# Eight tiles of routing logits computed at attention's head, attention and dispatch in one block, transfers in another order, rows of x normed one pair later

## The chip, the cores and the metric

One NeuronCore of a Trainium2 chip runs the whole program. Its engines are TensorE (PE, with its weight loads shown as PEld), VectorE (DVE), ScalarE (ACT), GpSimd (POOL) and SyncE (SP, which here only issues DMAs). Each engine takes its own instructions strictly in order and waits on semaphores for the others. The metric is device time in microseconds, the median of several executions.

## The reference, cut to what matters

x is 4 x 2048 x 256 in float32. With xn = layernorm(x), the result is x + attention(xn) + soft_moe(xn).

```
# attention: 16 heads in 4 groups of keys and values, head size 16, causal
q, k, v = xn @ wq.T, xn @ wk.T, xn @ wv.T
att = softmax(mask(q . k / 4));  ctx = att . v;  out1 = ctx @ wo.T
# soft mixture of experts: 16 experts x 64 slots = 1024 slots
y        = layernorm(xn) * norm_g + norm_b
se       = (layernorm(slot_embeds) * slot_g + slot_b) * scale
logits   = y . se                            # per batch 2048 tokens x 1024 slots
dispatch = softmax(logits, over tokens);  combine = softmax(logits, over slots)
slots    = dispatch^T . y                    # 1024 x 256 per batch
eout     = (gelu(slots @ Wg + bg) * (slots @ Wu + bu)) @ Wd + bd
out2     = combine . eout
```

## The kernel before, in words

The program runs five stages: `project` (norms, q, k, v, and y transposed into `y_cols` in memory, with q, k, v and y_cols split into chunks of 512 tokens), `attend`, `dispatch`, `experts` and `combine`. Project, attend and dispatch each have a block of their own; at the end of a block all engines meet, and the next block begins with a jump on every engine (L152 after project, L698 after attend).

**Attend.** A group is one of 4 batches times one of 4 key and value groups, so there are 16. A group has 40 units (a chunk of 512 queries against 128 keys) and 160 maxes (matmuls of 128 queries x up to 512 keys, whose row maxima DVE reduces, L857 and L863; the exponents need them beforehand). A step is one unit of scores for 4 heads (L890), exponents on ACT (L809), the product with v two steps later (L932), and four maxes (L903) of the work 22 steps ahead (`LEAD`). The first 22 steps, -22 to -1, thus hold maxes alone: that is attention's head. Scores, maxes, the small transposes of the row maxima ("m", L909) and of the context ("c", L917) share a ring of seven PSUM banks, in order; PE may fill a bank once ACT or DVE has read what it held seven banks ago. At the head ACT fills unused rows of the queries and keys of groups 1 to 3 with zeros (L799, L801), and SP loads group 1 at step -6, group 2 at 6 and group 3 at 46.

**Dispatch.** The phases are L0, L1 (logits of batch 0 and 1), then for each batch the two halves of P (the sum over tokens), with L2 and L3 after P of batch 0 and 1. A tile of logits is 128 tokens x 1024 slots: 12 matmuls (L1246), because both operands are split into a high and a low part and three products are kept. ACT copies the tile out of PSUM (L1108), DVE takes its row maximum (L1166) and updates the column maximum (L1174), ACT makes the exponents over slots one tile later (L1081), and SP stores them to `slot_exps` (L1033). There are 16 tiles in a batch, 4 in a chunk of y_cols; three chunks fit (`RING`), SP loads the next one (L989), and POOL splits it into high and low (L1193, L1195). In the last six tiles of L1, L2 and L3, DVE also subtracts the column maximum from a half tile of the batch before (L1137), and ACT takes its exponent (L1061). ACT norms rows of x in pairs of tiles (L1071) for the P phases; four pairs fit.

The order is written out: `program(s)` gives the steps of attend and the lists in `dispatch` its phases. No scheduler reorders anything.

## Time and profile before

| | us |
|---|---|
| median of 3 runs | 2688.85 (2688.53 to 2691.77) |
| the profiled execution's own time | 2690.94 |
| its span, first to last instruction | 2689.2 |
| project | 0 to about 156 |
| attend | about 160.6 to 1758.5 |
| its head (maxes alone) | 160.6 to 203.9 |
| dispatch | 1761.0 to about 2206 |
| experts and combine | the rest |

The page gives PE as busy 96% of the span, DVE 76%, ACT 64%. Matmul ends are modelled, so PE at 9 or 10 tenths does not say that PE could do no more: a matmul's busy time includes its way through the array, and the start-to-start distance of matmuls is what tells their price. PEclk is the share of 2.4 GHz that was granted: 1.00 is 2.4 GHz, 0.50 is 1.2 GHz. A name in square brackets after an instruction is what it waited for.

### The profile page before, as it was taken

What the parts mean: (1) busy time and instruction counts of PE and PEld (TensorE: products, weight loads), DVE (VectorE), ACT (ScalarE), POOL (GpSimd) and SP (SyncE); (2) the same over time, 40 slices, a digit from 0 to 9 for tenths busy, and PEclk for the clock granted to TensorE, in tenths of its full rate; (3) what the DMA queues carried; (4) which work ended last, traced back from release to release, by engine and by line L of the source; (5) the groups of instructions that cost most, each with busy time, mean ns of one, the idle gap of its engine ahead of it and who ended that gap; (6) DMA issues with size and microseconds to landing.
All of it is one profiled execution on the core that took longest, in us unless ns stands there. A gap on an engine that the chain in (4) does not pass through costs nothing. (4 is left out here: it accounts for less than half of the span.)

```text
span 2689.2 us, 47797 instructions
## 1 busy us (share of the span) xinstructions
PE 2580.5 (96%) x16291; PEld 1541.4 (57%) x16291; DVE 2046.0 (76%) x4879; ACT 1728.3 (64%) x3510; POOL 429.8 (16%) x676
## 2 busy tenths in 40 slices
PE   7989999999999999999999999998989999999999
PEld 4444444444444444444444444367877888889999
DVE  8779989989999998998998898468475523356665
ACT  4577777778777777777777777867656651222221
POOL 6601111111111111111111111223130100100000
PEclk9968999999999999999999999999999999999999
DMA  7945423303312321330330000044333354545554
GB/s 255 309 116 64 54 34 45 45 11 42 45 21 30 45 33 17 45 45 6 45 45 6 8 8 29 9 174 173 125 130 145 102 187 141 172 155 194 194 192 150
DMA packets 175855, 245.10 MB, mean 91 GB/s; under 512 B 57205, under 2 KB 129017, under 8 KB 174105
## 3 DMA queue, kind: packets, MB, share of 16 engines
q1 hardware_dynamic: 160088, 227.73, 33.8%
q10 hardware_dynamic: 15552, 14.68, 1.8%
q8 instruction: 114, 1.87, 0.3%
q14 instruction: 101, 0.82, 0.1%
HBM read 156.21 MB, written 84.97 MB: 90 GB/s over the span
## 5 line engine op out<-in xcount | busy, mean ns | idle before, releaser
L809 ACT ACTIVATE att_pr<-att_ring 128x512 f32<-128x512 f32 (+3 forms) x2560 | 1174.3, 550 | 330.7 <-PE att_ring L890 323.8
L857 DVE TENSOR_REDUCE att_mx<-att_ring 128x1 f32<-128x512 f32 x1536 | 967.6, 680 | 75.5 <-PE att_ring L903 73.1
L903 PE MATMUL att_ring<-att_ks,att_qs 48*128 48x512 f32 (+3 forms) x1920 | 647.3, 422 | 16.3 <-ACT att_pr L809 6.8
L890 PE MATMUL att_ring<-att_qs,att_ks 64*128 64x512 f32 (+3 forms) x1920 | 576.3, 406 | 6.6 <-DVE att_mx L863 2.3
L890 PEld LDWEIGHTS att_ring<-att_qs,att_ks 64*128 64x128 f32 x1920 | 300.4, 186 | 401.8 <-DVE att_mx L857 145.2
L863 DVE CUSTOM_DVE_ANT_0 att_junk<-att_ring,w_causal 128x256 bf16<-128x256 f32 (+3 forms) x1024 | 466.1, 486 | 57.6 <-PE att_ring L903 31.2
L932 PE MATMUL att_acc<-att_pr,att_v 128*17 128x512 f32 (+3 forms) x3840 | 453.8, 544 | 2.7 <-ACT att_cT L820 1.5
L903 PEld LDWEIGHTS att_ring<-att_ks,att_qs 48*128 48x128 f32 x1920 | 307.1, 185 | 142.1 <-ACT att_pr L809 103.5
L760 POOL TENSOR_SCALAR_AFFINE_SELECT att_pr<-att_pr 128x512 f32<-128x512 f32 x256 | 162.5, 635 | 1031.4 <-ACT att_pr L809 1031.4
L903 PE MATMUL att_ring<-g_ks,g_qs 48*128 48x512 f32 (+3 forms) x640 | 227.7, 467 | 15.5 <-PEq L152 5.8
L1513 ACT CAST com_e1h<-com_tp 128x1024 fp32r<-128x1024 f32 x64 | 64.7, 1016 | 236.3 <-PE com_tp L1573 236.3
L890 PE MATMUL att_ring<-g_qs,g_ks 64*128 64x512 f32 (+3 forms) x640 | 199.5, 412 | 2.2 <-DVE att_mx L863 0.8
L1589 PE MATMUL com_mp<-pre_parts,com_e1h 128*128 x1024 | 186.4, 283 | 4.1 <-DVE com_e1l L1538 4.1
L890 PEld LDWEIGHTS att_ring<-g_qs,g_ks 64*128 64x128 f32 x640 | 104.3, 189 | 135.7 <-DVE att_mx L857 51.7
L1589 PEld LDWEIGHTS com_mp<-pre_parts,com_e1h 128*128 128x128 f32 x1024 | 158.5, 190 | 4.9 <-issue 4.9
L932 PE MATMUL att_acc<-att_pr,g_v 128*17 128x512 f32 (+3 forms) x1280 | 151.5, 545 | 0.0
L903 PEld LDWEIGHTS att_ring<-g_ks,g_qs 48*128 48x128 f32 x640 | 111.3, 203 | 67.6 <-ACT att_pr L809 28.2
L1589 PE MATMUL com_mp<-pre_parts,com_e1l 128*128 x512 | 144.7, 283 | 0.0
L932 PEld LDWEIGHTS att_acc<-att_pr,att_v 128*17 128x17 f32 x3840 | 78.2, 118 | 112.7 <-ACT att_pr L809 76.4
L1246 PE MATMUL dis_ps<-w_seTh,w_yTh 128*128 128x512 f32 x256 | 105.9, 414 | 20.1 <-ACT dis_lg L1108 9.1
L1263 PE MATMUL dis_ps<-dis_y,pre_parts 128*128 128x257 f32 x512 | 112.6, 381 | 4.4 <-ACT pre_parts L1061 4.4
L1263 PE MATMUL dis_ps<-dis_y,dis_lg 128*128 128x257 f32 x512 | 113.5, 384 | 3.0 <-ACT dis_lg L1061 3.0
(170 smaller groups left out, 3271.1 us busy)
## 6 DMA issues: line engine op xcount, KB each, us to landing
slot_exps<-dis_e SPq DMA_DIRECT2D x64, 512.0 KB, 2.7
com_e<-slot_exps SPq DMA_DIRECT2D x64, 512.0 KB, 3.5
att_qs<-q_parts SPq DMA_DIRECT2D x72, 256.0 KB, 12.0
q_parts<-proj_part SPq DMA_DIRECT2D x32, 512.0 KB, 5.0
dis_y<-in_L_attn_x_dram SPq DMA_DIRECT2D x64, 256.0 KB, 2.8
att_ks<-k_parts SPq DMA_DIRECT2D x72, 128.0 KB, 12.7
y_cols<-proj_yT SPq DMA_DIRECT2D x16, 512.0 KB, 5.3
context<-att_cn SPq DMA_DIRECT2D x64, 128.0 KB, 2.0
```

The lines of the kernel that those rows point to most:

```text
L760: nc.gpsimd.affine_select(out=blk, in_=blk, compare_op=ALU.is_ge, fill=0.0, base=0, pattern=[[0, GS], [1, P]], channel_multiplier=-1).then ...
L809: nc.scalar.activation(pr[:, s % NPR, h, off:CH], spot(("s", s, h)), ACT.Exp, scale=float(HD) ** -0.5).then_inc(exp_done, 1)
L857: nc.vector.tensor_reduce(dst, spot(e), AX.X, ALU.max).then_inc(mb_used, 1)
L863: nc.vector.tensor_tensor_reduce(junk[:, h % 2, 0:wd], spot(e), w["causal"][:, CH - wd:CH], 1.0, LOW, ALU.add, ALU.max, dst).then_inc(mb_u ...
L890: nc.tensor.matmul(spot(e), ks[g][r, kb * P:(kb + 1) * P], qs[g][r, c, hf * CH + off:(hf + 1) * CH], start=True, stop=True).then_inc(sT_re ...
L903: nc.tensor.matmul(spot(e), qs[g][r, c, q0:q0 + P], ks[g][r, j * CH:j * CH + wd], start=True, stop=True).then_inc(mb_ready, 1)
L932: last = nc.tensor.matmul(acc[VW * h:VW * h + HD + 1, off:CH], v[bg % NKV][:, kb // TPC, :, kb % TPC], pr[:, n % NPR, h, off:CH], start=(n ...
L1246: last = nc.tensor.matmul(ps[:, i % 2, 2 * (t % 2) + h, :], lhs[:, n % RING, k, (t % TPC) * P:(t % TPC + 1) * P], w[rhs][:, k, h * 512:(h ...
L1263: last = nc.tensor.matmul(ps[:, i % 2, q, 0:D + 1], lgs[b % 2][:, t, (hf * HB + q) * P:(hf * HB + q + 1) * P], y[:, m % NY, t % 2, 0:D + 1 ...
L1513: nc.scalar.copy(e1h[:, q].rearrange("p s n -> p (s n)"), tp[:, q, 0:2, :].rearrange("p a n -> p (a n)")).then_inc(e1h_kept, 1)
L1589: last = nc.tensor.matmul(mp[:, q, 0:D], lhs[:, q, s, :], rhs[:, b, s, :], start=(s == 0 and rhs is eoh and lhs is e1h), stop=(s == SB - 1 ...
```

## The change

Six things change together.

1. **Eight tiles at the head.** The first 8 tiles of L0 (`NE`), in 16 halves of 128 x 512, are computed in steps -17 to -2 of attend, one half at the end of each step: six matmuls into one bank of the ring. ACT copies the half into a slot of `pr` and issues its store to a new array `first_logits`. Before that, SP loads two chunks of y_cols and POOL splits them. ACT's zeros are cut into pieces of 2048: six before the steps, twelve more one behind each of the halves 0 to 11. ACT waits for the first 12 stores at step 0 and for the last 4 at step 3.
2. **Their maxima.** In the last group SP loads the eight tiles back, to where dispatch wants them; DVE does their row and column maxima in attend's last 28 steps, where no maxes are left. L0 of dispatch then has tiles 8 to 15 only.
3. **One block.** Attend and dispatch share a block. In place of the meeting of all engines PE waits for each bank's last reader, and ACT waits before its third exponent tile until the contexts are stored.
4. **Exponents.** The 32 exponent tiles of L0 and L1 are spread over the 24 tiles of logits that are left, with four buffers in place of two.
5. **Transfers.** The loads of groups 1 and 2 move from steps -6 and 6 to -2 and 10, and the first waits until the first 12 halves are stored. In dispatch the chunk of y_cols is loaded after the exponents of a chunk's fourth tile are stored, no longer before those of its third.
6. **Rows of x** are normed one pair later in the P phases. The queries of all groups lie in one tensor, which project's `part` now shares.

```diff
+NE = 8
-    FIRST_LOADS = {-6: 1, 6: 2, 46: 3}
+    FIRST_LOADS = {-2: 1, 10: 2, 46: 3}
+    NL = 2 * NE
+    L_FROM = -LEAD + 5
+    L_LATE = NL - GS
...
+        early = [("l", s - L_FROM)] if 0 <= s - L_FROM < NL else []
-        out = [st[0], xs[0], st[1], xs[1]] + ev + [xs[2], st[2], st[3], xs[3]] + av
+        out = [st[0], xs[0], st[1], xs[1]] + ev + [xs[2], st[2], st[3], xs[3]] + early + av
...
 # SP
+            for n in range(NEC):
+                sp.dma_start(cols["low"][:, n].bitcast(F32), scr["yT_in"][0, n]).then_inc(cols["in"][n], 16)
                 for s in ALL_STEPS:
                     if s in FIRST_LOADS:
+                    sp.wait_ge(l_out, 16 * L_LATE)
                         load_first(FIRST_LOADS[s])
...
+                if s == STEPS - NU + AV_LAG:
+                    sp.wait_ge(pv_done, (NBG - 4 + -(-NE // 4)) * NU)
+                    for t in range(NE):
+                        sp.dma_start(lg[:, t, :], scr["first_logits"][t]).then_inc(l_in, 16)
...
 # ACT
+            for k in range(NRG * ZP):
+                zero_rows(k)
                 for s in ALL_STEPS:
+                for e in program(s):
+                    if e[0] == "l":
+                        act.wait_ge(mb_ready, turn[e] + 1)
+                        nc.scalar.copy(half_tile(e[1]), spot(e)).then_inc(l_kept, 1)
+                        if e[1] < (NKV - 2) * NRG * ZP:
+                            zero_rows(NRG * ZP + e[1])
+                        act.dma_start(scr["first_logits"][t, :, h * 512:(h + 1) * 512],
+                                      half_tile(e[1])).then_inc(l_out if e[1] < L_LATE else l_late, 16)
+                if s == 0:
+                    act.wait_ge(l_out, 16 * L_LATE)
+                if s == NPR - 1:
+                    act.wait_ge(l_late, 16 * (NL - L_LATE))
...
 # PE
+                    elif e[0] == "l":
+                        wait_bank(pe, e)
+                        pe.wait_ge(l_split, 2 * (t // TPC) + 2)
+                        for k in range(DK):
+                            nc.tensor.matmul(spot(e), hi, seTh[:, k, to], start=(k == 0), stop=False)
+                            nc.tensor.matmul(spot(e), hi, seTl[:, k, to], start=False, stop=False)
+                            last = nc.tensor.matmul(spot(e), lo, seTh[:, k, to], start=False, stop=(k == DK - 1))
...
 # dispatch
+        first_tile = lambda b: 0 if b else NE
+        SLOTS = 2 * TPB - NE
+        exps_by = lambda b, t: min(-(-2 * TPB * (b * TPB + t + 1 - NE) // SLOTS), b * TPB + t)
...
-                            norm_rows(half_of(ph) * PAIRS + (t + 1) // 2 + 2)
+                            norm_rows(half_of(ph) * PAIRS + (t + 1) // 2 + 1)
```

On PE at the head, steps -19 to -14, where `att_ring` is a bank of the ring: before,

```order
L903 MATMUL att_ring<-g_ks,g_qs 128x512 x2
L903 MATMUL att_ring<-g_ks,g_qs 128x256 x2
L903 MATMUL att_ring<-g_ks,g_qs 128x512 x6
L909 MATMUL att_ring<-w_ident,att_nml 32x128
L903 MATMUL att_ring<-g_ks,g_qs 128x384 x2
```

and now, the maxes being L977, the first transpose of row maxima L994 and a half tile of logits the six matmuls L986 to L988:

```order
L977 MATMUL att_ring<-g_ks,w_queries 128x512 x4
L986 MATMUL att_ring<-w_seTh,w_yTh 128x512
L987 MATMUL att_ring<-w_seTl,w_yTh 128x512
L988 MATMUL att_ring<-w_seTh,w_yTl 128x512
L986 MATMUL att_ring<-w_seTh,w_yTh 128x512
L987 MATMUL att_ring<-w_seTl,w_yTh 128x512
L988 MATMUL att_ring<-w_seTh,w_yTl 128x512
L977 MATMUL att_ring<-g_ks,w_queries 128x512 x2
L994 MATMUL att_ring<-w_ident,att_nml 32x128
L977 MATMUL att_ring<-g_ks,w_queries 128x384 x2
```

Six matmuls stand behind the four maxes of each step from -17 on, and the transpose stands behind the first half tile.

On ACT, from attend's first instruction: before, all zeros and then the first exponents,

```order
L799 CAST att_qs<-w_causal 32x4096
L801 CAST att_ks<-w_causal 32x2048
L799 CAST att_qs<-w_causal 32x4096
L801 CAST att_ks<-w_causal 32x2048
L799 CAST att_qs<-w_causal 32x4096
```

and now, where L840 are the zeros, L848 the copy of a half tile and L853 its store:

```order
L840 CAST w_queries<-w_causal 32x2048 x2
L840 CAST att_ks<-w_causal 32x2048
L840 CAST w_queries<-w_causal 32x2048 x2
L840 CAST att_ks<-w_causal 32x2048
L848 COPY att_pr<-att_ring 128x512
L840 CAST w_queries<-w_causal 32x2048
L853 DMA first_logits<-att_pr 128x512
L848 COPY att_pr<-att_ring 128x512
L840 CAST w_queries<-w_causal 32x2048
L853 DMA first_logits<-att_pr 128x512
```

A copy that frees a bank of the ring stands behind a piece of zeros twelve times.

On PE where attend ends and dispatch begins, before:

```order
L932 MATMUL att_acc<-att_pr,att_v 17x512 x4
L917 MATMUL att_ring<-w_ident,att_cT 128x128 x4
L698 UNCONDITIONAL_BRANCH
L1211 UNCONDITIONAL_BRANCH
L1246 MATMUL dis_ps<-w_seTh,w_yTh 128x512
```

and now:

```order
L1017 MATMUL att_acc<-att_pr,att_v 17x512 x4
L1002 MATMUL att_ring<-w_ident,att_cT 128x128 x4
L1348 UNCONDITIONAL_BRANCH
L1385 MATMUL dis_ps<-w_seTh,w_yTh 128x512
```

The end of the block has gone; a jump within the block is left. The first matmul of dispatch is now that of tile 8.

## Rows read from the trace of the kernel before

**Rows 1.** The page's busy times by engine.

```profile
PE 2580.5 (96%) x16291; PEld 1541.4 (57%) x16291; DVE 2046.0 (76%) x4879; ACT 1728.3 (64%) x3510; POOL 429.8 (16%) x676
```

**Rows 2.** Busy time of each engine by stretch, around attention's head.

```profile
core 0: us, PE busy (x) PEld busy (x) DVE busy (x) ACT busy (x) POOL busy (x), PEclk, DMA share, GB/s
...
200.00:205.00 5.00, 4.99 (x11) 2.41 (x10) 5.00 (x13) 0.31 (x1) 0.00 (x0) 0.50 1.11 126
...
215.00:220.00 5.00, 5.00 (x36) 2.30 (x33) 5.00 (x14) 3.97 (x9) 0.63 (x1) 0.90 0.02 5
```

**Rows 3.** Timeline of the head's first part: start, duration, instruction, wait.

```profile
160.59 3.60 ACT L799 CAST att_qs<-w_causal 32x4096 fp32r<-32x4096 f32 x1 [4.99 <-PEq L152]
...
164.10 1.89 ACT L801 CAST att_ks<-w_causal 32x2048 fp32r<-32x2048 f32 x1
...
169.04 0.20 POOL L778 CAST att_nml<-att_nm 128x16 fp32r<-128x16 f32 x1 [8.21 <-DVE att_nm L831]
```

**Rows 4.** Timeline of the head's second part and of step 0.

```profile
170.68 0.39 PE L909 MATMUL att_ring<-w_ident,att_nml 128*32 128x128 f32 x1
...
190.72 2.46 DVE L857 TENSOR_REDUCE att_mx<-att_ring 128x1 f32<-128x512 f32 x4
...
192.14 0.40 SPq L528 DMA_DIRECT2D att_qs<-q_parts  x1
...
203.89 0.76 PE L890 MATMUL att_ring<-g_qs,g_ks 64*128 64x512 f32 x1
```

**Rows 5.** Timeline where attend ends and dispatch begins.

```profile
1755.71 0.58 ACT L820 COPY att_cT<-att_acc 128x512 f32<-128x512 f32 x1 [1.19 <-PE att_acc L932]
1756.44 0.63 PE L917 MATMUL att_ring<-w_ident,att_cT 128*128 128x128 f32 x4 [0.80 <-ACT att_cT L820]
...
1761.02 0.77 PE L1246 MATMUL dis_ps<-w_seTh,w_yTh 128*128 128x512 f32 x1 [3.95 <-PEq L698]
...
1761.58 0.63 PE L1246 MATMUL dis_ps<-w_seTl,w_yTh 128*128 128x512 f32 x1
...
1762.01 0.63 PE L1246 MATMUL dis_ps<-w_seTh,w_yTl 128*128 128x512 f32 x1
...
1766.01 0.40 PE L1246 MATMUL dis_ps<-w_seTh,w_yTh 128*128 128x512 f32 x1
...
1766.71 0.40 PE L1246 MATMUL dis_ps<-w_seTh,w_yTh 128*128 128x512 f32 x1
```

**Rows 6.** Timeline of L0: one tile's period on ACT and DVE.

```profile
1777.41 1.01 ACT L1108 COPY pre_parts<-dis_ps 128x1024 f32<-128x1024 f32 x1 [0.65 <-PE dis_ps L1246]
...
1778.32 1.15 ACT L1081 ACTIVATE dis_e<-pre_parts,dis_nr 128x1024 f32<-128x1024 f32 x1
...
1779.37 0.19 ACT L1081 ACTIVATION_READ_ACCUMULATOR dis_e<-pre_parts,dis_nr 128x1 f32 x1
...
1780.21 1.02 ACT L1108 COPY pre_parts<-dis_ps 128x1024 f32<-128x1024 f32 x1 [0.65 <-PE dis_ps L1246]
...
1790.80 3.37 DVE L1174 TENSOR_TENSOR dis_cm<-dis_cm,pre_parts 128x1024 f32<-128x1024 f32 x1
```

**Rows 7.** Busy times by stretch: attend's end, and L0.

```profile
1720.00:1730.00 10.00, 8.46 (x72) 2.89 (x68) 0.00 (x0) 10.00 (x25) 3.51 (x4) 1.00 0.00 1
...
1780.00:1790.00 10.00, 10.00 (x44) 8.05 (x43) 8.66 (x8) 7.84 (x11) 3.50 (x2) 1.00 0.66 259
```

**Rows 8.** DMA issues, whole run: queue, count, KB, median us to landing.

```profile
slot_exps<-dis_e SPq DMA_DIRECT2D x64, 512.0 KB, 2.7
...
w_yTl<-y_cols SPq DMA_DIRECT2D x16, 512.0 KB, 4.2
...
proj_x<-in_L_attn_x_dram ACTq DMA_DIRECT2D x12, 512.0 KB, 5.3
```

**Rows 9.** DMA issues between 160 and 230.

```profile
context<-att_cn SPq DMA_DIRECT2D x1, 128.0 KB, 15.0
```

**Rows 10.** Waits between 1862 and 1980: us in total, times, longest.

```profile
ACT dis_y L1071 <- DMA dis_y<-in_L_attn_x_dram: 13.6, 10, 2.0
```

More of the change, by code:

```diff
@@ L99, in project @@
         x = a.sb("x", [P, NX, TPC, D])
+        room = queries[:, QW:]
+        part = room[:, 0:12 * CH].rearrange("p (q s h n) -> p q s h n", q=2, s=3, h=2)
         xn = a.sb("xn", [P, 2, TPC, D])
@@ L537, in load_ones, with attend @@
             yield sp.dma_start(ks[row:row + 1, :].bitcast(F32), w["ones"][0:S // 64, :].bitcast(F32)).then_inc(ones_set, 16)
-def attend(nc, w, scr, g0, cols):
+def attend(nc, block, w, scr, g0, cols, queries, first_logits):
     def chunk_units(c):
@@ L642, in place @@
             spot[1] += need
-        return where, before, {e: m[-1] for e, m in mates.items()}
+        return where, before, {e: m[-1] for e, m in mates.items()}, held
     NEAR = 4
     fills = [e for s in ALL_STEPS for e in program(s) if e[0] != "a"]
-    where, before, last_mate = place(fills)
+    where, before, last_mate, held_last = place(fills)
     turn = {e: n for n, e in enumerate(e for e in fills if e[0] != "s")}
@@ L653, in attend @@
         passed = a.sem("passed")
-        qs = [g0["qs"]] + [a.sb(f"qs{g}", [P, CPB, HL * CH], F32R) for g in range(1, NKV)]
+        qs = [queries[:, g * QW:(g + 1) * QW].rearrange("p (c n) -> p c n", c=CPB) for g in range(NKV)]
         ks = [g0["ks"]] + [a.sb(f"ks{g}", [P, S], F32R) for g in range(1, NKV)]
@@ L942, in dispatch, with bank_free, stored @@
+        def bank_free(pe, bank):
+            if bank < NBANK:
+                wait_read(pe, held_last[bank])
+            else:
+                pe.wait_ge(cT_ready, NBG * CPB)
+        def stored(eng):
+            for c in range(CPB):
+                eng.wait_ge(c_out[c], 16 * NBG)
+        return bank_free, stored
+def dispatch(nc, block, w, io, scr, pre, cols, first_logits, before):
     HB = SB // 2
@@ L976, in dispatch @@
         NYP = B * 2 * PAIRS
+        first_tile = lambda b: 0 if b else NE
+        SLOTS = 2 * TPB - NE
+        exps_by = lambda b, t: min(-(-2 * TPB * (b * TPB + t + 1 - NE) // SLOTS), b * TPB + t)
+        WIDE = 2 * TPB
+        place = lambda n: n % 4 if n < WIDE else n % 2
+        stores_before = lambda n: n // 4 if n < WIDE else (WIDE // 4) + (n - WIDE) // 2
         def tiles_of(m):
@@ new lines, in _, with split, column_maxes @@
+        @block.gpsimd
+        def _(pool):
+            def split(n):
+                if n < B * CPB:
+                    q = n % RING
+                    wait_apart(pool, yT_in[q], 16 * ((n - NEC) // RING), passed)
+                    nc.gpsimd.tensor_copy(yTh[:, q], yTl[:, q].bitcast(F32)).then_inc(yT_high, 1)
+                    pool.wait_ge(yT_high, n - RING - NEC + 1)
+                    nc.gpsimd.tensor_tensor(yTl[:, q], yTl[:, q].bitcast(F32), yTh[:, q].bitcast(F32),
+                                            ALU.subtract).then_inc(yT_split, 1)
+            def column_maxes(b):
+                wait_apart(pool, cm_done, TPB * (b + 1), passed)
+                for hf in range(2):
+                    h = slice(hf * 512, (hf + 1) * 512)
+                    nc.gpsimd.partition_all_reduce(cm[:, b % 2, h], cm[:, b % 2, h], P, RMAX).then_inc(ca_ready, 1)
+            for b in range(B):
+                if b:
+                    column_maxes(b - 1)
+                for n in range(b * CPB if b else NEC, b * CPB + CPB):
+                    split(n + RING)
+            column_maxes(B - 1)
@@ L1640, in block_kernel @@
                 "in": [a.sem(f"yT_in{n}") for n in range(RING)]}
+        first_logits = {"nr": a.sb("nr", [P, 2, TPB]), "cm": a.sb("cm", [P, 2, NS]),
+                        "nr_ready": a.sem("nr_ready"), "cm_done": a.sem("cm_done")}
+        with ExitStack() as place:
+            parts = Alloc(nc, place, "pre").sb("parts", [P, 2, B, SB, D], F32R)
+        lg = parts[:].bitcast(F32).rearrange("p a b s d -> p (a b s d)").rearrange("p (t n) -> p t n", n=NS)
+        first_logits["lg"] = lg
+        both = ExitStack()
         with ExitStack() as early:
             b = Alloc(nc, early, "w")
+            queries = b.sb("queries", [P, NKV * QW], F32R)[:]
             w["causal"] = b.sb("causal", [P, CH])
@@ L1650, in block_kernel @@
                 load_ones(sp, w, g0["ks"], g0["ones_set"]))
-            project(nc, w, io, scr, g0)
-            attend(nc, w, scr, g0, cols)
+            project(nc, w, io, scr, g0, queries)
+            block = both.enter_context(nc.Block())
+            before = attend(nc, block, w, scr, g0, cols, queries, first_logits)
         with ExitStack() as late:
             b = Alloc(nc, late, "pre")
-            parts = b.sb("parts", [P, 2, B, SB, D], F32R)
+            b.sb("place", [P, 2 * B * SB * D])
             high, low = parts[:, 0].bitcast(F32), parts[:, 1].bitcast(F32)
@@ L1670, in block_kernel @@
                    "parts": parts}
-            dispatch(nc, w, io, scr, pre, cols)
+            with both:
+                dispatch(nc, block, w, io, scr, pre, cols, first_logits, before)
             com = combine_inputs(late, nc, io, scr)
```

1055 lines of the change are left out of this document (552 added, 503 removed).

## The prediction

> **What bounds the kernel now.** I read the page's busy times first [rows 1]: PE is busy 96% of the span. That is an average; what eight tiles are worth where they stand now, and what they cost where they go, has to be read at those two places.
>
> The first is L0. In the timeline [rows 6] ACT's copies of two tiles in a row start at 1777.41 and 1780.21, and each ends a wait on PE of 0.65. So a tile takes 2.80 us and PE sets it: 12 matmuls, one each 0.233 (the 13th and the 16th matmul of dispatch start at 1766.01 and 1766.71, 0.70 for three) [rows 5]. ACT's part of a tile is a copy of 0.91 (1777.41 to 1778.32) and exponents of 1.24 (1778.32 to 1779.56), together 2.15. DVE is busy 8.66 of 10 us there [rows 7].
>
> The second is attention's head. In the stretches [rows 2] DVE is busy 5.00 of 5 us between 200 and 205 while the granted clock is 0.50, the 1.2 GHz level; PE reads 4.99, but with only 11 matmuls in 5 us, each waiting for DVE to read a bank. DVE needs 2.46 for four full maxes [rows 4]. So at the head DVE sets the time and PE, at half clock, has room. Between 215 and 220 the clock comes back (0.90) once scores, maxes and products stand close together. The third place is the border of attend and dispatch [rows 5]: the last transposes end at 1757.07, and dispatch's first matmul starts at 1761.02 after 3.95 us in which PE's sequencer waited at the block's end. From there the clock is at half again: matmuls two and three start 0.43 apart (1761.58, 1762.01).
>
> **The change part by part.**
>
> *Taken out of L0.* Eight tiles by 2.80 = 22.4 us, all on the path, since PE sets L0.
>
> *The border.* Without the meeting PE goes on at 1757.07 when it has had its transposes; the banks it fills first were read by exponents that are over by then. 1761.02 - 1757.07 = 3.9 us. At least a jump remains, so between 0 (the engines' sequencers need the time anyway) and 3.9; I take 3.9, as nothing else is shown in the gap. The first tile's 12 matmuls took 4.99 (1761.02 to 1766.01) in place of 2.80; with no gap in PE's work the clock should stay: 2.2 us more, or 0 if the short waits at attend's end bring it down all the same. So dispatch gives back 22.4 + 3.9 + 2.2 = 28.5.
>
> *The exponents of L0 and L1.* 32 tiles over 24 is 4/3 a tile: ACT 0.91 + 4/3 x 1.24 = 2.56 a tile, still under 2.80. A tile with two exponents takes 3.39 on ACT, its neighbours 2.15, and PE has two tiles of PSUM to run ahead in. Cost 0, but the cover has shrunk from 0.65 to 0.24 us a tile. The stores grow to 512 KB every 2.1 us while the DMA engines are 0.66 busy [rows 7], about 0.85; with four buffers and 2.7 us to landing [rows 8] that holds. Bounds: 0 to 0.5 a tile over 16 tiles, 8 us.
>
> *Maxima of the eight tiles.* 16 operations on DVE of the kind that took 3.37 beside POOL [rows 6] and about a third of it alone, some 20 to 30 us with POOL beside a few of them, in a stretch where DVE is busy 0.00 of 10 and ACT 10.00 [rows 7]. Hidden. Behind them on DVE stands one copy of row maxima, for a chunk of scores four steps later. The load back, 4 MB, is issued in the last group's first steps, some 16 steps before DVE's maxes run out. 0, at most 2.
>
> *The head, the term that costs.* Before, the m transpose, behind 26 maxes, starts at 170.68 and step 0, behind 88, at 203.89 [rows 4]: 62 maxes in 33.2 us, 2.14 a step of four. Now:
> - Half tile 0 comes before that transpose, at half clock: 6 x 0.43 = 2.6 us.
> - The next step is ten matmuls at half clock, 4.3, so 2.2 more than 2.14. By then PE has worked without a gap for about as long as in dispatch's first tile, where the clock was back after 5 us [rows 5], and I take full clock from there.
> - 14 more steps. PE at full clock needs 10 x 0.233 = 2.33 at most. ACT, in ten of the 14, has a copy of 0.58 (the same shape) [rows 5] and a piece of zeros of 1.76 to 1.89 (3.51 from 160.59 to 164.10 for 4096 columns; 1.89 for 2048) [rows 3], together 2.4. DVE's share stays 2.14. So 2.4 against 2.14: 14 x 0.26 = 3.6.
> - POOL's two splits (a cast and a subtraction each) stand before its part in the m transpose, which it did at 169.04 [rows 3]. They begin when the chunk is there, about 4.2 us after 160.6 [rows 8]. PE needs the first split at about 169.5, where half tile 0 stands. 0 to 3 us; I take 0, since PE at half clock is late there anyway.
> Sum 2.6 + 2.2 + 3.6 = 8.4. Below, it can't be under 14 x (2.33 - 2.14) = 2.7; above, see the first rival. In return steps 0 to 5 run at full clock. They lie before 216 with DVE nearly always busy [rows 2]: 0 to 2.5 us back, I take 1.5.
>
> *Other moves.* Group 1's load was issued at 192.14 [rows 4], is now issued about 15 us later, and is needed at step 18, so 18 steps of 2.14 or more after step 0: hidden. The later norming takes ACT's waits for rows of x away (13.6 us in ten waits) [rows 10], in phases where PE was busy throughout; against that, three pairs in place of two are normed in the middle of L2 and L3. 0, between -2 and 2. The chunk of y_cols loaded one tile later still has two chunks' time: 0.
>
> Sum: -28.5 + 8.4 - 1.5 = -21.6. From the profiled execution, 2690.94 (span 2689.2), that is 2669.3; it was 2.1 above the median 2688.85, so 2667.
>
> The Trainium skill speaks against the head term: TensorE: Matmul & The Clock Gate, in "A second HAM failure mode: psum-queue depth-cycling", says that a PE which idles briefly between groups of matmuls as it goes round PSUM banks can have its clock swing between the two levels. The trace agrees for the head as it was (0.50 with 4.99 of 5 us busy) and not for attend as a whole, where the same ring runs at 1.00 in the stretches shown of its end [rows 7]. By that rule the head would be the first rival.
>
> **The rivals.**
> - *The clock stays at half through the head; slower.* For it: at the head it was 0.50 though PE read busy for 4.99 of 5 us, and PE still waits for ACT and DVE once a step [rows 2]. Against: at half clock ten matmuls need 4.3 us and nothing else needs more, so PE would have no gap, and without gaps it came back within 5 us at 1761 [rows 5]. Price: 16 steps of 4.3 in place of 2.14 is 34.6, and nothing back in steps 0 to 5: -28.5 + 34.6 = +6, 2695. It decides from about 14 of the 16 steps at half clock.
> - *ACT holds up the head's end.* The last four halves are stored while group 1's load runs; a context store of 128 KB took 15.0 us to land in such a stretch [rows 9], and ACT waits for these four at step 3. With 15 to 20 us to landing step 3 waits some 10: 2677. For: these rows. Against: that store stood in SP's own queue, and on ACT's queue 512 KB landed in 5.3 [rows 8]. The Trainium skill, DMA: Bandwidth & Descriptors, "Queues, rings and completion order", says that a DMA engine takes turns between queues packet by packet; by that the wait is 0, and no row here shows both at once for these shapes.
> - *ACT or the stores become the bound of L0 and L1.* 3.3 a tile in place of 2.8 over 16 tiles: +8, 2675. For: cover of 0.24 us only, DVE 87% busy. Against: four buffers.
> - *The border stays.* A jump and fetching of instructions cost the 3.9, and the clock falls as before, 2.2: 2673.
> - *The head hides nearly all.* 2.7 in place of 8.4: 2661.
>
> **How the numbers follow.** Forecast 0.50 at 2667, its own range 2662 to 2673. Half clock at the head 0.07; late stores 0.09; L0 and L1 bound elsewhere 0.12; the border 0.09; the head hidden 0.13. The range of 2656 to 2680 takes in the last three and most of the stores, and leaves the first out. A measurement of this kernel tells 0.2% (5.4 us) from no change: under 2683.5 is faster. All but the first rival lie below it; for several of them at once I move some chance: faster 0.87, within 0.2% 0.05, slower 0.08.
>
> **What would show it.** In the profile after: the granted clock in 5 us stretches from 169 on, 0.50 until about 175 and then near 1.00; the first score matmul at 211 to 213 (before 203.89); ACT's copies of half tiles 2.4 apart; no wait of ACT at step 3. Dispatch's first matmul within 0.5 us of attend's last transposes, at full clock, about 7 us later on the clock of the span than 1757; tiles of L0 2.80 apart; the first matmul of P some 22 us earlier than before. The prediction is wrong if the head's end lies past 220, or if the tiles of L0 are more than 3 us apart.

## The result, and the profile after

The changed kernel takes 2676.5 us (median of 7 runs, 2669.35 to 2685.1); the kernel before, run beside it, 2688.85 (7 runs, 2686.45 to 2691.77). The ratio is 0.9954, with a 95% interval of 0.9939 to 0.9968: faster by 0.46%, about 12 us. The forecast was 2667; 2676.5 lies inside the range of 2656 to 2680, but 9.5 us above the likeliest case. The profiled execution has a span of 2677.9 against 2689.2, 11.3 less, and all readings below are of these two. The page's busy times, against [rows 1]:

```profile
span 2677.9 us, 47844 instructions
PE 2569.2 (96%) x16291; PEld 1530.4 (57%) x16291; DVE 2037.7 (76%) x4879; ACT 1729.7 (65%) x3524; POOL 428.3 (16%) x676
```

As before they name no culprit. The span has to be cut at events that both kernels have: ACT's first piece of zeros, step 0's first score, attend's last transposes, dispatch's first matmul, the first and the last product.

| stretch | before | after | difference | forecast |
|---|---|---|---|---|
| to the first zeros | 160.6 | 161.0 | +0.4 | 0 |
| head: to step 0's first score | 43.3 | 48.5 | +5.2 | +8.4 |
| steps of attend, to the end of the last transposes | 1553.2 | 1565.3 | +12.1 | -1.5 |
| border, to dispatch's first matmul | 3.95 | 0.48 | -3.5 | -3.9 |
| L0 and L1, to the first product | 99.5 | 78.9 | -20.6 | -24.6 |
| first to last product (both P of 0 to 3, L2, L3) | 343.3 | 337.4 | -5.9 | 0 |
| the rest | 485.3 | 486.3 | +1.0 | 0 |

One row is off by 13.6 us, and against it all others together are 3.3 us better than forecast: the head and the products gave more (3.2 and 5.9), L0 and L1 4.0 less. The timeline of that stretch (start, duration, engine, line, and in brackets the idle time before it and what ended it) answers to [rows 4]:

```profile
209.46 0.43 PE L964 MATMUL att_ring<-w_queries,g_ks 64*128 64x512 f32 x1
...
226.44 0.94 ACT L865 ACTIVATE att_pr<-att_ring 128x256 f32<-128x256 f32 x3 [9.04 <-DMA first_logits<-att_pr]
...
226.97 0.76 PE L964 MATMUL att_ring<-w_queries,g_ks 64*128 64x512 f32 x1 [6.21 <-ACT att_pr L865]
```

Step 0 starts at 209.46, 5.6 later than before. Then ACT waits 9.04 us for stores of half tiles, and PE waits for ACT. The stretches around it answer to [rows 2] (busy time, instructions, granted clock, DMA share, GB/s):

```profile
core 0: us, PE busy (x) PEld busy (x) DVE busy (x) ACT busy (x) POOL busy (x), PEclk, DMA share, GB/s
210.00:215.00 5.00, 4.22 (x17) 2.11 (x17) 4.99 (x15) 2.95 (x8) 0.64 (x1) 0.96 1.01 160
215.00:220.00 5.00, 5.00 (x25) 1.95 (x22) 4.08 (x10) 1.92 (x5) 1.69 (x4) 0.50 1.04 184
220.00:225.00 5.00, 0.75 (x10) 0.16 (x8) 1.53 (x4) 0.00 (x0) 0.00 (x0) 0.50 1.06 157
225.00:230.00 5.00, 3.03 (x13) 1.30 (x17) 1.98 (x4) 2.79 (x7) 0.63 (x1) 0.50 0.39 28
```

Between 220 and 225 every compute engine stands still or nearly so; only the DMA engines work. The clock was at half before that, from 215, where PE had 25 matmuls in 5 us and mostly waited for DVE's maxes. The last four stores of half tiles (ACT's queue, from 204.4 to 209.7), as the trace has them:

```profile
L853 ACTq DMA_DIRECT2D first_logits<-att_pr x4: 326/334/346, 204.4 to 209.7; - x4
  ACT att_pr L865: 9.0, 1
DMA to landing us min/median/max: 6.6/13.5/16.7
```

The border answers to [rows 5]:

```profile
1774.17 0.63 PE L1002 MATMUL att_ring<-w_ident,att_cT 128*128 128x128 f32 x4 [0.80 <-ACT att_cT L876]
1774.84 0.39 ACT L832 COPY att_cc<-att_ring 128x272 f32<-128x272 f32 x1 [0.81 <-PE att_ring L1002]
1775.28 0.50 PE L1385 MATMUL dis_ps<-w_seTh,w_yTh 128*128 128x512 f32 x1 [0.48 <-ACT att_cc L832]
1775.62 0.40 PE L1385 MATMUL dis_ps<-w_seTl,w_yTh 128*128 128x512 f32 x1
1775.85 0.39 PE L1385 MATMUL dis_ps<-w_seTh,w_yTl 128*128 128x512 f32 x1
```

The meeting is gone and the matmuls are 0.23 apart from the second on. What is left, 0.48, is a wait that the prediction did not name: the first matmul needs the bank that ACT's copy reads (the prediction had the first banks free by then). In L1, at 1820 to 1829:

```profile
1820.38 1.02 ACT L1243 COPY dis_lg<-dis_ps 128x1024 f32<-128x1024 f32 x1 [0.65 <-PE dis_ps L1385]
...
1823.57 4.04 ACT L1193 ACTIVATE dis_y<-dis_y,w_yb,w_ys 128x256 f32<-128x256 f32 x8
1827.51 0.99 ACT L1243 COPY dis_lg<-dis_ps 128x1024 f32<-128x1024 f32 x1
...
1828.56 0.50 PE L1385 MATMUL dis_ps<-w_seTh,w_yTh 128*128 128x512 f32 x1 [2.61 <-ACT dis_lg L1243]
```

The tiles ahead of it are on average as in [rows 6], 2.80 apart (copies at 1809.18 and 1811.98); a tile with two exponents takes 3.19 and the one behind it 2.41. These two copies are 7.13 us apart: between them two exponents and the four pairs of rows of x in one piece, and PE waits 2.61 for it.

### The profile page after: what moved, and what is told of

Its sections match the earlier page's. It is cut to its first block and busy times, and to the rows that moved or that the text cites. A ratio compares the mean times of both kernels' runs of the same rounds, so it can differ in the third digit from the quotient of the medians.

```text
span 2677.9 us, 47844 instructions
## 1 busy us (share of the span) xinstructions
PE 2569.2 (96%) x16291; PEld 1530.4 (57%) x16291; DVE 2037.7 (76%) x4879; ACT 1729.7 (65%) x3524; POOL 428.3 (16%) x676
## 5 line engine op out<-in xcount | busy, mean ns | idle before, releaser
L977 PE MATMUL att_ring<-att_ks,w_queries 48*128 48x512 f32 (+3 forms) x1920 | 647.4, 422 | 16.9 <-ACT att_pr L865 8.1
L964 PE MATMUL att_ring<-w_queries,att_ks 64*128 64x512 f32 (+3 forms) x1920 | 576.5, 407 | 7.4 <-DVE att_mx L937 2.3
L964 PEld LDWEIGHTS att_ring<-w_queries,att_ks 64*128 64x128 f32 x1920 | 300.8, 186 | 403.5 <-DVE att_mx L931 144.6
L977 PEld LDWEIGHTS att_ring<-att_ks,w_queries 48*128 48x128 f32 x1920 | 307.2, 185 | 142.5 <-ACT att_pr L865 103.8
L977 PE MATMUL att_ring<-g_ks,w_queries 48*128 48x512 f32 (+3 forms) x640 | 212.7, 440 | 11.5 <-PEq L156 5.8
L964 PE MATMUL att_ring<-w_queries,g_ks 64*128 64x512 f32 (+3 forms) x640 | 200.2, 413 | 9.0 <-ACT att_pr L865 6.2
L964 PEld LDWEIGHTS att_ring<-w_queries,g_ks 64*128 64x128 f32 x640 | 104.4, 189 | 144.0 <-DVE att_mx L931 54.0
L977 PEld LDWEIGHTS att_ring<-g_ks,w_queries 48*128 48x128 f32 x640 | 101.3, 193 | 58.6 <-ACT att_pr L865 28.2
L1385 PE MATMUL dis_ps<-w_seTh,w_yTh 128*128 128x512 f32 x224 | 92.9, 415 | 19.9 <-ACT dis_lg L1243 13.0
## 6 DMA issues: line engine op xcount, KB each, us to landing
w_queries<-q_parts SPq DMA_DIRECT2D x96, 256.0 KB, 12.1
```

What stands on the lines that cost most here:

```text
L964: nc.tensor.matmul(spot(e), ks[g][r, kb * P:(kb + 1) * P], qs[g][r, c, hf * CH + off:(hf + 1) * CH], start=True, stop=True).then_inc(sT_re ...
L977: nc.tensor.matmul(spot(e), qs[g][r, c, q0:q0 + P], ks[g][r, j * CH:j * CH + wd], start=True, stop=True).then_inc(mb_ready, 1)
L1385: last = nc.tensor.matmul(ps[:, i % 2, 2 * (t % 2) + h, :], lhs[:, n % RING, k, (t % TPC) * P:(t % TPC + 1) * P], w[rhs][:, k, h * 512:(h ...
```

## The experiments

There are twelve kernels. "Early load" in the later ones is the edit of the second. Behind "Measured" stand the median, the lowest and highest run, and the ratio to the kernel before with its 95% interval; the kernel before had 2689.1, 2689.5 and 2690.2 in the three sets. Theory A, for the row that is off by 13.6: the last four stores stand behind group 1's load on the DMA engines, ACT waits, and PE's clock is back late.

A stretch is read from one execution of each kernel, and kernels with the same code in a stretch show how far that can be trusted. The steps of attend, by what each kernel does there:

| attend | step 0's first score to step 20's | all steps |
|---|---|---|
| as before (before, e4_before_norm1) | 51.0, 51.0 | 1553.2, 1558.6 |
| with ACT's wait at step 3 (changed, e3_norm2, e5_two_blocks, e8_yT_order) | 60.7, 57.9, 58.0, 59.1 | 1565.3, 1560.0, 1563.5, 1563.2 |
| without it (the other eight) | 50.3 to 54.2 | 1550.6 to 1558.9 |

All steps differ by 5 us within one row; the first twenty tell the three rows apart. So the wait and the half clock behind it cost the changed kernel 9.7 of its 12.1, and 7 to 8 in the other three, where ACT waited 8.1, 8.2 and 6.6. The other 2.4 lies behind step 20, where short pieces of half clock fall differently in each execution (13.6 us at 0.50 against 10.3 before).

**e1_hold.** The load held back until the stores have landed.

```
                 if s in FIRST_LOADS:
                     sp.wait_ge(l_out, 16 * L_LATE)
+                    sp.wait_ge(l_late, 16 * (NL - L_LATE))
                     load_first(FIRST_LOADS[s])
```


> The changed kernel, but SP also waits for the last four stores of halves before it issues group 1's load (the load starts some 8 us later). Theory A (the stores queue behind that load): the last four stores land in 2 to 5 us, ACT's wait of 9.04 us before step 3 goes, step 3 no longer stands still at 222 to 226, attend's end comes 9 to 12 us earlier, about 2667. Rival B (stores of 256 KB from ACT's queue take about 15 us whatever runs beside them): the wait stays at 8 to 10 us, 2676. Rival C (the wait goes, but the clock is at half through steps 0 to 10 in any case, since DVE bounds them): the wait goes and only 5 to 7 us come back, 2670.

Measured: 2671.75 (2664.16 to 2677.98), ratio 0.9932 (0.9906 to 0.9957). The last four stores, and the stretches after step 0:

```profile
L854 ACTq DMA_DIRECT2D first_logits<-att_pr x4: 326/326/327, 202.9 to 208.2; - x4
DMA to landing us min/median/max: 2.0/2.1/2.5
```
```profile
215.00:220.00 5.00, 5.00 (x30) 1.80 (x30) 4.08 (x11) 2.27 (x7) 1.19 (x4) 0.50 1.11 121
220.00:225.00 5.00, 4.96 (x25) 1.67 (x23) 3.76 (x9) 3.21 (x7) 0.51 (x1) 0.67 0.95 104
225.00:230.00 5.00, 5.00 (x37) 2.32 (x36) 4.85 (x11) 4.46 (x11) 0.64 (x1) 1.00 1.13 125
```

The same 256 KB from the same queue land in 2.1 us in place of 13.5: rival B (15 us whatever runs beside) falls. The wait is gone, and attend's steps take 1552.7 in place of 1565.3. The first twenty steps give back 8.7 of that (52.0 against 60.7); the other 3.9 lies behind them, where the code is the same, in short pieces of half clock. The clock falls to 0.50 at 215 here too, as rival C has it, and is back at 1.00 after 225, where with the wait it was still 0.50. The median moved by 4.8, to 2671.75: theory A had the cause right and its 9 to 12 us were too much, and rival C, with 5 to 7 us and 2670, came nearest to the time. Single runs of one kernel are 14 us apart.

**e2_early_load.** The load ahead of the late stores.

```
-    FIRST_LOADS = {-2: 1, 10: 2, 46: 3}
+    FIRST_LOADS = {-14: 1, 10: 2, 46: 3}
                 if s in FIRST_LOADS:
-                    sp.wait_ge(l_out, 16 * L_LATE)
                     load_first(FIRST_LOADS[s])
```


> The changed kernel, but group 1's load is issued at step -14 instead of -2 and does not wait for the stores, so it runs beside stores 2 to 11 and the last four stores have the DMA engines to themselves. Theory A: those early stores land late (10 to 17 us) but nobody waits for them before step 0; the wait before step 3 goes, 9 to 12 us earlier, about 2667. Rival B (stores always take 15 us): 2676. Rival D: the wait only moves, to step 0, where ACT waits for twelve stores: 2 to 6 us there, 2671.

Measured: 2671.69 (2665.4 to 2676.69), ratio 0.9931 (0.9909 to 0.9952). No wait at step 3, none at step 0 (rival D falls); the stores around step 0 land in 2.0 at the median and 4.9 at most; all steps take 1555.5, the first twenty 50.6. Two different edits that part stores and load do the same.

**e11_in_turn.** Stores and load at the same time, but a short backlog.

```
+                for i, _ in enumerate(itertools.chain(load_group(...), load_ones(...))):
+                    if g == 1 and i % 3 == 2:
+                        sp.wait_ge(loaded[g], 16 * (i + 1))
```


> The changed kernel, but SP has at most three transfers of group 1's load under way: it waits for each three to land before it issues the next. Theory A1 (a store waits for all that is queued on the DMA engines ahead of it, whichever queue it came from): with a short backlog the late stores land in 2 to 7 us although the load still runs beside them, ACT's wait before step 3 goes, 2667 to 2671. Theory A2 (the engines share packet by packet between the two queues for as long as both have work): the load runs beside them as before, the stores take 10 us or more, the wait stays at 5 to 10 us.

Measured: 2671.3 (2664.67 to 2674.51), ratio 0.9924 (0.9909 to 0.9939). Landing of the last four stores, and the stretches in which load and stores are both under way:

```profile
L855 ACTq DMA_DIRECT2D first_logits<-att_pr x4: 326/326/326, 205.0 to 210.3; - x4
DMA to landing us min/median/max: 2.1/3.7/6.8
```
```profile
210.00:215.00 5.00, 4.21 (x18) 2.08 (x15) 5.00 (x12) 2.70 (x6) 0.64 (x1) 0.94 0.82 159
215.00:220.00 5.00, 5.00 (x26) 2.05 (x23) 4.23 (x12) 2.44 (x7) 1.70 (x4) 0.50 0.69 105
220.00:225.00 5.00, 4.93 (x38) 2.31 (x36) 4.80 (x12) 3.90 (x9) 0.64 (x1) 0.88 0.64 92
```

Two of these four stores were issued before the load began and landed in 2.3 and 2.1; the two beside it, with three transfers under way, landed in 6.8 and 5.2, in place of 12.5 to 16.7. ACT does not wait, step 3 goes on, and the first twenty steps take 52.2. So what made the stores late was how much SP had issued, 17 transfers in ten us, though it stood in another queue.

A1's 2 to 7 us came and A2's 10 or more did not. But that does not settle how the engines divide their time between the queues, since beside a short load a shared engine is soon free too, and the packets speak for each theory in turn. In the changed kernel, between 215 and 222, the load's queue (q1) and that of the stores (q10) moved the same number of packets (packets, MB, share of 16 engines' time):

```profile
q1 hardware_dynamic: 235, 0.81, 68.9%
q10 hardware_dynamic: 239, 0.45, 34.4%
```

That is A2, packet by packet: the load's packets are the larger ones and take most of the time, and the stores move 0.45 MB in 7 us, where in e11_in_turn they moved 0.48 MB in the 2 us before the load (206 to 208). But in e11_in_turn, between 208 and 212, the store issued at 208.0 hardly moves while the three transfers issued ahead of it do, which is A1:

```profile
q1 hardware_dynamic: 160, 0.59, 103.0%
q10 hardware_dynamic: 4, 0.01, 1.0%
```

So a store can wait for what was issued ahead of it, and it can share the engines with the load. What decides between the two stays open.

**e5_two_blocks.** The border alone undone.

```
-            with both:
+            both.close()
+            with nc.Block() as block:
                 dispatch(nc, block, ...)
```


> The changed kernel with attend and dispatch in two blocks again, as before; all else as changed. If the border term was sized right: 3.5 to 4 us between attend's last transposes and the first matmul of logits in place of 0.5, and 2.2 us more in the first tile at half clock, so 5 to 6 us slower than the changed kernel, about 2682. Rival: a jump costs the same in one block and the gain came from the eight tiles alone: within 1 us in the stretch from the last transposes to the third tile.

Measured: 2681.17 (2675.3 to 2692.78, 12 runs), ratio 0.9972 (0.9958 to 0.9987), 4.7 above the changed kernel.

```profile
1771.71 0.63 PE L1002 MATMUL att_ring<-w_ident,att_cT 128*128 128x128 f32 x4 [0.80 <-ACT att_cT L876]
...
1774.59 0.77 PE L1385 MATMUL dis_ps<-w_seTh,w_yTh 128*128 128x512 f32 x1 [2.26 <-PEq L1821]
1775.15 0.63 PE L1385 MATMUL dis_ps<-w_seTl,w_yTh 128*128 128x512 f32 x1
1775.58 0.63 PE L1385 MATMUL dis_ps<-w_seTh,w_yTl 128*128 128x512 f32 x1
```

The meeting costs 2.26 here (less the 0.48 of the joined block 1.8 net), less than the 3.95 before: the block's end no longer waits for the context's last store, since SP's wait for it now stands in dispatch. Before, that store was issued at 1758.50 and landed at 1760.47, and PE went on 0.55 later; here it was issued at 1773.77 and PE went on at 1774.59, before it landed at 1775.64. And the matmuls are 0.43 apart, the clock at half: the first twelve take 5.26 against 2.91, 2.4 more. 1.8 + 2.4 = 4.2, and the medians say 4.7. (L0 and L1 as a whole take 81.6 against 78.9, but seven kernels with the same code there lie between 76.9 and 81.7, so that stretch does not show it.) The border is real, and its price in the kernel before had three parts, of which one was the wait for a store. The joined block does not always keep the clock: in e10_all, e11_in_turn and e12_early_norm2 it was at half there as well, without a meeting, and the first twelve matmuls took 3.8 to 3.9.

**e8_yT_order.** The chunks of y_cols loaded where they were.

```
+                        if t % TPC == TPC - 2:
+                            load_yT(b * CPB + t // TPC + RING)
                         store_exps(exps_by(b, t) if b < 2 else b * TPB + t + 1)
-                        if t % TPC == TPC - 1:
-                            load_yT(b * CPB + t // TPC + RING)
```


> The changed kernel with the chunks of y_cols loaded where they were before, one tile earlier and ahead of the exponents' stores. The prediction priced this move at 0 with two chunks of time in hand. If so: within 1.5 us of the changed kernel in the stretch of L0 and L1 and in L2 and L3. If SP now waits for a chunk's last tile with finished exponents behind it: ACT waits for free buffers in L0 and L1, 2 to 6 us slower.

Measured: 2677.03 (2672.15 to 2678.37), ratio 0.995 (0.9931 to 0.9968); L0 and L1 78.6 (78.9), first to last product 337.5 (337.4). No effect, as forecast.

**e3_norm2, e12_early_norm2, e4_before_norm1.** The later norming: undone in the changed kernel, undone with the early load, and done alone in the kernel before.

```
-                            norm_rows(half_of(ph) * PAIRS + (t + 1) // 2 + 1)
+                            norm_rows(half_of(ph) * PAIRS + (t + 1) // 2 + 2)
```


> The changed kernel with the rows of x normed two pairs ahead again, as before. The phases from the first product to the last logits took 5.9 us less after the change than before. If the later norming is worth that (ACT no longer waits for rows of x in front of exponents that PE needs): 3 to 6 us slower than the changed kernel. If it comes from another part (which cores of the block's queue, clock): within 1.5 us of it.

> The kernel with group 1's load issued early, and the rows of x normed two pairs ahead as before the change. The profile of the changed kernel with that (343.4 us from the first to the last product, against 337.4) said 6 us, its median 2678 against 2676.5 said 2. If the later norming is worth 5 to 6: that stretch takes 340 or more against 334.4, and the median is 2675 to 2678. If it is worth 2 or less: the stretch is under 338 and the median 2671 to 2674.

> The kernel before with only the norming of rows of x one pair later. If the later norming is worth 3 to 6 us by itself: 2683 to 2686. If not: 2687 to 2690. If it only helps together with the new order of transfers, this run is at 2689 while the run without it is slower than the changed kernel.

| kernel | pairs ahead | median | first to last product |
|---|---|---|---|
| changed | 1 | 2676.5 | 337.4 |
| e3_norm2 | 2 | 2678.28 | 343.4 |
| e2_early_load | 1 | 2671.69 | 334.4 |
| e12_early_norm2 | 2 | 2672.21 | 339.2 |
| before | 2 | 2689.09 | 343.3 |
| e4_before_norm1 | 1 | 2689.47 | 342.2 |

With two pairs ahead the stretch is longer in each pair of rows, by 6.0, 4.8 and 1.1; the medians differ by 1.8, 0.5 and -0.4, and the interval of the last (0.9977 to 1.0007) holds no change. Part of the difference between the profiles is where short pieces of half clock fell in that one execution: in e1_hold, with the same code there, the stretch is 338.3. One part of it is free of that: the P phases of batches 2 and 3, at full clock in every run, take 115.6 or 115.7 in the three kernels with two pairs ahead and 114.7 in all nine with one (e9_skew and e10_all, which change more, left out), e4_before_norm1 too. So 1.0 us is shown. What the later norming is worth in the other phases, up to 6 us in all, these runs don't settle. ACT's waits for rows of x over that stretch (us in total, times, longest; the first part of it before stands in [rows 10], the whole had 56.9 in 43 waits) do shrink, but most of what went was not on the path:

```profile
ACT dis_y L1193 <- DMA dis_y<-in_L_attn_x_dram: 38.0, 30, 2.1
```

**e7_zeros_pool.** ACT's part of the head moved.

```
-                        if e[1] < (NKV - 2) * NRG * ZP:
-                            zero_rows(NRG * ZP + e[1])
+                    if m < 2:            # GpSimd, behind its parts of the first two m
+                        for k in range(NRG * ZP * (m + 1), NRG * ZP * (m + 2)):
+                            ...
+                            nc.gpsimd.tensor_copy(rows, w["causal"][r, 0:1].to_broadcast([32, S])).then_inc(zeroed[g], 1)
```


> The kernel with group 1's load issued early, and the twelve pieces of zeros that stand behind half tiles 0 to 11 on ACT moved to GpSimd. If ACT (copy and zeros) sets the head's steps at 2.53 us: steps become 2.33 (ten matmuls at full clock), and step 0's first score comes about 2.4 us earlier. If matmuls with their waits set them: the spacing of the half tiles stays at 2.5. If GpSimd beside DVE makes DVE's maxes slower: 2.6 or more.

Measured: 2668.17 (2660.64 to 2670.28), ratio 0.9911 (0.9889 to 0.9933). From the second half tile's copy to the last one: changed kernel 175.9 to 209.1, 33.2, with eleven spacings of 2.53; here 177.1 to 208.8, 31.7. The 2.53 was ACT's (copy, zeros and the issue of a store), but when the zeros end PE is up to 1.5 us ahead in its banks, and the next copies follow 1.0 and 2.0 apart: only 1.5 us were on the path. The head as a whole was not shorter (48.7 from first zeros to first score against 48.5), since in this execution the clock stayed at half through 175 (0.50 in 170:175, 0.65 in 175:180; changed kernel 0.63 and 1.00). The early load, with the same late clock, had 50.1.

**e6_spread_norms.** The 4.04 us in one piece divided.

```
-                        if b >= 1 and t == 7:
-                            norm_rows(2 * (b - 1) * PAIRS + NY)
+                        if b >= 1 and t < 8 and t % 2:
+                            norm_rows(2 * (b - 1) * PAIRS + (t + 1) * NY // 8)
```


> The kernel with group 1's load issued early, and in L1 the four pairs of rows of x normed one at a time behind tiles 1, 3, 5 and 7 in place of all four behind tile 7. If those 4.04 us in one piece, on an ACT that is 96% busy there, are what lost 4 us in L0 and L1: the stretch from the first matmul of logits to the first product takes 76 to 77 us in place of 80 to 81, and the run is some 4 us under the one with the early load alone, 2668. If ACT's work as a whole is the bound there (exponents of 32 tiles behind 24 tiles): the stretch stays within 1 us of 80.

Measured: 2669.29 (2666.29 to 2672.17), ratio 0.9925 (0.9906 to 0.9943). L0 and L1 take 77.7 against 80.3 with the early load alone. That is inside the spread of kernels with the same code there (76.9 to 81.7), but the place shows it: from the tenth copy behind dispatch's first matmul to the eighteenth it is 23.7 in place of 26.0. So 2.3 of the 4 us that were missing, and the medians say 2.4.

The last six tiles of L1 remained, 4.5 us apart in every kernel, and before the change as well. One period in the changed kernel:

```profile
1838.91 0.99 ACT L1243 COPY dis_lg<-dis_ps 128x1024 f32<-128x1024 f32 x1
...
1839.94 1.22 DVE L1303 TENSOR_REDUCE w_nr<-dis_lg 128x1 f32<-128x1024 f32 x1 [1.60 <-ACT dis_lg L1243]
1841.08 1.21 DVE L1311 TENSOR_TENSOR w_cm<-w_cm,dis_lg 128x1024 f32<-128x1024 f32 x1
1842.21 0.69 DVE L1272 TENSOR_TENSOR pre_parts<-pre_parts,w_cm 128x512 f32<-128x512 f32 x1
1842.93 0.63 ACT L1183 ACTIVATE pre_parts<-pre_parts 128x512 f32<-128x512 f32 x1 [1.88 <-DVE pre_parts L1272]
1843.46 0.99 ACT L1243 COPY dis_lg<-dis_ps 128x1024 f32<-128x1024 f32 x1
```

Neither engine is full: DVE idles 1.60 for ACT and ACT 1.88 for DVE, in turn. The exponents of the slots (L1183) need this tile's subtraction on DVE, and stand on ACT ahead of the next tile's copy.

**e9_skew.** Those exponents one tile later.

```
-                        if b >= 1 and t >= TPB - AHEAD:
-                            exp_tile(b - 1, t - (TPB - AHEAD))
+                        if b >= 1 and t > TPB - AHEAD:
+                            exp_tile(b - 1, t - (TPB - AHEAD) - 1)
...
                         token_exps(b * TPB + TPB)
+                        exp_tile(b - 1, AHEAD - 1)
```


> The kernel with group 1's load issued early, and in the last six tiles of L1, L2 and L3 the exponents of the slots on ACT stand one tile later, behind the next tile's copy. In L1 these tiles stand 4.5 to 4.6 us apart, while ACT has some 3.4 and DVE 3.4 a tile: copy, then DVE's two maxima and its subtraction, then exponents, then the next copy, one behind the other. If that loop sets them: 3.4 to 3.6 apart, 5 to 6 us less in each of L1, L2 and L3, and the run at 2654 to 2658. If the clock (0.66 in the stretches 1827:1832 and 1837:1842 of such a kernel) sets them: still 4.5 apart, 2671.

Measured: 2648.98 (2647.2 to 2651.77), ratio 0.9847 (0.9833 to 0.9862), 22.7 under the early load alone.

```profile
1829.75 1.00 ACT L1242 COPY dis_lg<-dis_ps 128x1024 f32<-128x1024 f32 x1
...
1831.36 0.68 DVE L1272 TENSOR_TENSOR pre_parts<-pre_parts,w_cm 128x512 f32<-128x512 f32 x1
...
1832.08 0.63 ACT L1182 ACTIVATE pre_parts<-pre_parts 128x512 f32<-128x512 f32 x1 [0.19 <-DVE pre_parts L1272]
1832.61 1.00 ACT L1242 COPY dis_lg<-dis_ps 128x1024 f32<-128x1024 f32 x1
```

The copies are 2.86 apart in place of 4.55. L0 and L1 take 70.2 (80.3), first to last product 323.2 (334.4): 21.3 together, more than the 15 to 18 expected. In L2 and L3 both kernels are at full clock, so that the loop alone gave the 3.6 (49.4 against 53.0) and 4.2 (47.9 against 52.1) there; in L1 it gave 10.1, with 6.8 us at half clock gone as well. The rival named the clock as the cause; it came back with the loop's end. From 1829.2 to 1843.2 it is 1.00, where the changed kernel has 0.88.

**e10_all.** Early load, zeros on GpSimd, divided norms, later exponents.

> Group 1's load early, the twelve pieces of zeros on GpSimd, the four pairs in L1 normed one at a time, and the exponents of the slots one tile later. If the parts add: 1.5 (zeros), 2 (pairs) and 15 (exponents) under the 2671.7 of the early load alone, about 2653. If the pairs' gain is the same slack of ACT that the later exponents free: 2655 to 2657.

Measured: 2643.92 (2640.11 to 2645.87), ratio 0.9828 (0.9814 to 0.9842): the best version, 1.7% under the kernel before and 32.6 us under the changed one. L0 and L1 take 70.0, as with the later exponents alone, so the divided norms add nothing to them. It is 5 us under e9_skew, whose values, 2647.2 to 2651.77, don't meet these. The profiled executions are 8.9 apart, and that lies in attend: the head takes 46.1 in place of 48.8, and the steps 1550.6 in place of 1557.0. In the steps e10_all was at half clock for 11.2 us and e9_skew for 27.3. In e2_early_load and e12_early_norm2, with the same attention code as e9_skew, 20.5 and 28.1 us at half clock go with 1555.5 and 1558.9, which is 0.4 to 0.5 us for each; at that price the clock is the whole difference of the steps. The early load's two kernels agree: 13.7 us at half clock and 1551.8 with the zeros on GpSimd, 20.5 and 1555.5 with them on ACT. Whether the zeros on GpSimd keep the clock or chance did stays open.

## Why the prediction was right, and where it was wrong

- **Direction and range** were right, on the terms of L0 and the border. The likeliest case was not what happened: it was the second rival. That its 2677 met 2676.5 is in part luck: the row of attend's steps came out 3.6 above that rival's sum and L0 and L1 4.0 above it, and the head and the products made up for it by 3.2 and 5.9.
- **The step that failed** is the late stores, "on ACT's queue 512 KB landed in 5.3": the prediction made of it a wait of 0. The choice between that row and the 15.0 of a store in such a stretch [rows 9] went to the row with the same queue, not to the one with the same load. The row is of loads of x in project, and its 5.3 is a median of two kinds: the six issued with at most three of SP's transfers under way landed in 3.7 to 4.3, the six with five to nine in 6.3 to 11.4. So the trace before already showed that a queue of its own does not protect a transfer. The rival had the place (ACT at step 3) and the price of the wait: some 10, measured 9.04 (6.6 to 8.2 in three other kernels with it). From the page's rule that was weighed against it (the Trainium skill, DMA: Bandwidth & Descriptors, "Queues, rings and completion order": engines take turns between queues packet by packet) the prediction drew a wait of 0. The turns are there from 215 to 222 (235 and 239 packets); the wait of 0 does not follow, since a store then moves at the pace of the load's larger packets, 0.45 MB in 7 us. A short backlog saved the stores in e11_in_turn, a queue of their own did not.
- **Steps 0 to 5 at full clock**, -1.5: without the wait all steps came out at -0.5 and +2.3 (1552.7 and 1555.5 against 1553.2), and the first twenty at +1.0 and -0.4 (52.0 and 50.6 against 51.0). The prediction took the clock to be kept. It reads 0.96 in 210:215, where PE has 17 matmuls and DVE is busy 4.99 of 5 us, and 0.50 from 215 on, before any wait of ACT. The rule that was weighed for the head (the Trainium skill, TensorE: Matmul & The Clock Gate, "A second HAM failure mode: psum-queue depth-cycling": the clock can swing where PE idles briefly as it goes round its banks) agrees with the fall at 215 and not with the head, 1.00 from 175 to 210.
- **The head**: 8.4 forecast, 5.2 measured. Half tile 0 cost its 2.6 as forecast (from the first zeros to the transpose of row maxima 12.7 against 10.1). The next step took PE 2.1 (halves at 174.2 and 176.3) in place of 4.3, as the clock was back before it; that is most of the 3.2. In e2_early_load, e7_zeros_pool and e8_yT_order it came back one step later, and the copies of the first two halves are 4.5 apart in place of 2.9. The 14 steps behind it took 33.1, 2.37 each, against 33.6 forecast: ACT's 2.53 stood in eleven of them, and the ring of banks took up most of what ACT was behind (e7_zeros_pool, 1.5). The first rival (half clock throughout, 2695) fell at once: 1.00 from 175 on.
- **The border**: -3.9 and -2.2 forecast; e5_two_blocks gives 1.8 and 2.4, the wait for the context's last store is 1.7 of the 3.95, and 0.48 stayed.
- **Eight tiles**: -22.4, sized rightly (tiles 2.80 apart on average, as before). What L0 and L1 gave back short of it, 4, was half named in the third rival: the cover on ACT had gone. But it was no 0.5 a tile; it was the one piece of 4.04, which the prediction's sum of ACT's work leaves out (e6_spread_norms, 2.3). The rest, 1.7, is less than what executions of one code differ by there.
- **Other moves**: -5.9 in place of 0 with 2 on either side. 1.0 of it is shown to be the later norming; for the rest the three pairs of runs don't settle whether it is the norming or the clock.
- The signs given: dispatch's first matmul came 0.48 behind the transposes, as said, but 18 later than 1757 and not 7, and the first product came 6.3 earlier and not 22; step 0's first score came at 209.5, ahead of the 211 to 213 given. Group 1's load was issued at 203.9, 12 us later than before and not 15.

## What to carry to other kernels

When a transfer must land soon, look at what all queues have been given before it, not at its own alone; a row on landing times holds only for the backlog in which it was taken. Part such a transfer from a bulk load in time, or keep the bulk load short. And when two engines both show idle time that the other ends, in turn and in each period, look for the one instruction that stands a place too early: here moving one exponent behind the next copy gave 22.7 us, where the whole change gave 12. And before a stretch of one execution is used to size a cause, compare it between kernels that have the same code there: here such stretches differed by 5 us, about as much as most of the effects.

## What the runs showed of the hardware

- 256 KB from ACT's queue mostly took 2.0 to 2.5 us to land without transfers of SP's queue beside it (4.4 once, e1_hold at 200.4), 5.2 and 6.8 with three transfers of SP's queue under way, and 6.6 to 16.7 beside the whole load of group 1 (17 transfers, 2.5 MB, of which two to ten had been issued ahead of each store), with the DMA engines 1.01 to 1.06 busy at only 157 to 184 GB/s. The stores issued at 204.4, 205.4, 207.4 and 209.7 landed in 6.6, 12.5, 14.5 and 16.7, about when SP's transfers issued beside them did (SP's of 209.8 in 16.5).
- In the kernel before, 512 KB on ACT's queue landed in 3.7 to 4.3 us with at most three of SP's transfers under way, and in 6.3 to 11.4 with five to nine.
- With both queues at work the engines moved as many packets of one as of the other (235 and 239 from 215 to 222), so that the queue with the smaller packets got the smaller share, 0.45 MB of 1.26.
- PE's busy time does not tell its clock: it reads 5.00 of 5 us at 0.50 with 25 matmuls (215:220 of the changed kernel) and at 1.00 with 37 (225:230 of e1_hold).
- A meeting of the engines kept PE for 2.26 us when no store had to be waited for (0.48 without a meeting, 3.95 with a store), and the half clock behind it cost 2.4 more in the first twelve matmuls.
